# Order of the two GpSimd multiplies in each slot of a selective-scan kernel

## The reference, cut to what matters

```python
h = _L0_tok_ref(L0_tok_log_dt, L0_tok_Lambda, x, 1024)
h = jnp.concatenate([h, txt], axis=1)
# inside _L0_attn_ref, on the normalised h
dt = jax.nn.softplus(jnp.einsum('blr,dr->bld', dt_in, dt_proj_w) + dt_proj_b)
dA = jnp.exp(dt[..., None] * A)
dBx = dt[..., None] * B[:, :, None, :] * x[..., None]
h = dA_t * h + dBx_t                      # one step along the sequence
y = jnp.einsum('bdn,bn->bd', h, C_t)      # sum over the 16 states
y = jnp.moveaxis(ys, 0, 1) + D * x
```

## Time and profile before

| | us |
|---|---|
| median of 3 runs (6466.54 to 6470.77) | 6468.88 |
| the profiled execution, own time | 6470.72 |
| its span, first to last instruction | 6469.0 |
| busy in the span: PE / PEld / DVE / ACT / POOL | 5967.5 / 5445.7 / 5822.2 / 5225.1 / 5736.9 |
| mean granted TensorE clock | 0.966 |
| DMA: 478.57 MB, mean 74 GB/s | |

### The profile page before, as it was taken

How to read it: one execution, slowest core, us unless ns; L and a number is a source line. 1 busy time by engine, 2 the same in 40 slices (tenths; PEclk the granted TensorE clock), 3 DMA queues, 4 the chain that set the end, 5 groups by cost and what they waited for, 6 DMA issues and landing times. The chain is left out here.

```text
span 6469.0 us, 109402 instructions
## 1 busy us (share of the span) xinstructions
PE 5967.5 (92%) x33363; PEld 5445.7 (84%) x33363; DVE 5822.2 (90%) x4749; ACT 5225.1 (81%) x12983; POOL 5736.9 (89%) x3788
## 2 busy tenths in 40 slices
PE   4658689999999999999999999999999999999998
PEld 3433489999999999999999999999999999999997
DVE  7874599999999999999999999999999999999996
ACT  4536688888888888888888888888888888888885
POOL 2430599999999999999999999999999999999995
PEclk8769899999999999999999999999999999999999
DMA  2440121122221222221222212222212222112220
GB/s 56 97 94 0 63 76 70 68 77 85 85 74 64 79 80 84 85 72 66 74 85 85 79 61 77 79 85 84 74 64 79 79 85 84 67 66 79 85 79 32
DMA packets 96128, 478.57 MB, mean 74 GB/s; under 512 B 13089, under 2 KB 17329, under 8 KB 87410
## 3 DMA queue, kind: packets, MB, share of 16 engines
q1 hardware_dynamic: 95602, 471.63, 21.0%
HBM read 328.35 MB, written 143.24 MB: 73 GB/s over the span
## 5 line engine op out<-in xcount | busy, mean ns | idle before, releaser
L1079 POOL TENSOR_TENSOR s_ring<-s_bc,s_u_t 128x820 f32<-128x820 f32 x2048 | 3625.6, 1790 | 4.3 <-DMA s_bc<-rows_bc 4.3
L985 ACT ACTIVATE s_decay<-s_dt_t,a_neg 128x205 f32<-128x205 f32 x8192 | 3047.2, 420 | 428.9 <-DVE s_ring L1150 359.9
L882 PE MATMUL s_y_ps<-s_ring,ident 128*128 128x205 f32 x16384 | 3164.5, 343 | 142.8 <-POOL s_ring L1085 74.0
L882 PEld LDWEIGHTS s_y_ps<-s_ring,ident 128*128 128x128 f32 x16384 | 2888.4, 193 | 232.3 <-POOL s_ring L1085 139.1
L1144 DVE TENSOR_TENSOR_SCAN s_decay<-s_decay,s_ring 128x820 f32<-128x820 f32 x1216 | 2265.2, 1863 | 221.9 <-ACT s_decay L985 219.7
L1085 POOL TENSOR_TENSOR s_ring<-s_ring,s_bc 128x820 f32<-128x820 f32 x832 | 1607.3, 1932 | 55.4 <-DVE s_ring L1144 55.2
L1144 DVE TENSOR_TENSOR_SCAN s_ring<-s_decay,s_ring 128x820 f32<-128x820 f32 x832 | 1543.8, 1856 | 45.8 <-ACT s_decay L985 45.4
L915 PE MATMUL s_xch<-s_x_t,w_low 128*128 128x205 f32 x8192 | 1524.1, 338 | 0.5 <-ACT s_x_t L1025 0.2
L915 PEld LDWEIGHTS s_xch<-s_x_t,w_low 128*128 128x128 f32 x8192 | 1423.9, 190 | 32.7 <-issue 30.5
L1150 DVE TENSOR_TENSOR s_ring<-s_decay,s_bc 128x820 f32<-128x820 f32 x1216 | 1230.3, 1012 | 41.9
L307 POOL TENSOR_TENSOR t_mag<-t_mag,t_osc 128x512 f32<-128x512 f32 x128 | 167.1, 1342 | 273.0 <-ACT t_osc L293 273.0
(11 more groups left out here) (165 smaller groups left out, 4817.2 us busy)
## 6 DMA issues: line engine op xcount, KB each, us to landing
s_bc<-rows_bc SPq DMA_DIRECT2D x64, 3280.0 KB, 11.2
mixed<-t_res SPq DMA_DIRECT2D x32, 1024.0 KB, 10.0
s_x_in<-mixed SPq DMA_DIRECT2D x64, 512.0 KB
s_h<-mixed SPq DMA_DIRECT2D x64, 512.0 KB
before<-s_h SPq DMA_DIRECT2D x64, 512.0 KB
out<-s_h SPq DMA_DIRECT2D x64, 512.0 KB
s_x_in<-in_txt SPq DMA_DIRECT2D x64, 308.0 KB
s_h<-in_txt SPq DMA_DIRECT2D x64, 308.0 KB
```

Source lines behind the costliest of these rows:

```text
L882: last = nc.tensor.matmul(y_ps, ident[:, :], ring[:, c % RING, n * LEN:(n + 1) * LEN], start=False, stop=(c % 4 == 3 and n == CN - 1))
L985: last = A.activation(decay[s % 2][:, n * LEN:(n + 1) * LEN], dt_t[:, par, j, :], ACT.Exp, scale=t["a_neg"][:, j, n0 + n:n0 + n + 1])
L1079: nc.gpsimd.tensor_tensor(ring[:, s % RING, :].rearrange("p (n l) -> p n l", n=CN), bc[:, par, n0:n0 + CN, :], u_t[:, j, :].unsqueeze(1).b ...
```

## The change

Inside GpSimd's `chunk` the two parts of a slot change places: the product with C of chunk `s-3` is issued first, the inputs of chunk `s` second. The stages of `POOL_PLAN` still follow both. Nothing else is touched: the same instructions with the same operands and waits, in another order on one engine.

```diff
             def chunk(u, par, s, x, scan, after):
-                if scan:
-                    inputs(u, par, s)
                 if (s - LAG) % CHUNKS not in ON_DVE:
                     if s >= LAG and scan:
                         times_c(u, par, s - LAG)
                     if s < LAG and after:
                         times_c(u - 1, 1 - par, s - LAG + CHUNKS)
+                if scan:
+                    inputs(u, par, s)
```

## The result

The changed kernel takes **6493.74 us** (median of 14 runs, 6475.03 to 6512.86), the kernel before 6466.75 in 14 runs beside it: ratio 1.0038, 95% interval 1.0029 to 1.0048. It is 27 us slower (19 to 31 by the interval), where the prediction said 6482 (6464 to 6503), 13.6 us slower. The direction is the one forecast, and the waits that were forecast grew as they should; but as far as the traces tell, they are the smaller part of the loss. The larger part is something that the prediction did not have.

A forecast was written before the change was run, and what follows sets the result against it. Four nearly full engines, in a chain without slack through GpSimd, TensorE, ScalarE and VectorE, were taken as the bound. Late stages add 0.28 and 0.16 us, 0.44 per pair; 31 pairs give 13.6, so 6468.9 becomes 6482 (6464 to 6503).

The forecast's parts named there:

- the exits: GpSimd's product with C of chunk 18, in the even and odd entry, for which TensorE waits 0.57 and 0.19 us.
- the count of 22 steps: On GpSimd, 22 steps of inputs stand between products 28 and 18 before and after, so nothing is won there.
- `root2` 1.75 later in the even entry: GpSimd's norm stage in slot 17 gets one more step of inputs ahead of it, 1.75 us.
- ScalarE takes up 0.43: After the late shift, ScalarE's wait of 0.33 and overlap of 0.10 absorb 0.43 us, leaving 1.32 of lateness.
- Scan 3's lead: Even entry: chunk 3's inputs end 3.60 us before its scan; 3.64 new lateness may make VectorE wait 0.04 to 0.1.
- the rival of 6503: VectorE starves for late inputs at scan 3 of the even entry, up to 34 us slower; chance 0.11.
- 0.44 us a pair: Lengthening of each pair of entries from both late products of chunk 18; 13.6 us over 31 pairs.
- The 0.28 of the even entry: Lateness in us reaching GpSimd's product of chunk 18 and TensorE in the even entry.
- the 0.16 of the odd entry: Lateness in us reaching TensorE in the odd entry: 0.51, of which wait and overlap take up 0.35.
- No instruction is added or removed: Whole kernel: no DMA and no queue but GpSimd's is touched; one wait moves ahead of the inputs.
- The forecast's own band: Whole kernel's time under the main forecast, 6474 to 6492 us; chance 0.57.
- The rival "no change": GpSimd, busiest, gets no more work and ScalarE's 14% idle time takes up the lateness: 6469 us; chance 0.24.

The follow-up runs named there:

- e3: Kernel before, with the product with C issued ahead of the inputs in slots 5 to 15 alone; 6539.6 us, ratio 1.0117.
- e4: Kernel before, with the product with C issued ahead of the inputs in slots 29 to 31 and 0 to 3 only; 6532.0 us, ratio 1.0105.
- e1: Changed kernel with `root2` moved one slot earlier in GpSimd's plan, from slot 17 to 16; 6491.0 us, ratio 1.0038.
- e8: Changed kernel with TensorE's loop alone written out over 20 entries, 3 passes in place of 30; 6475.0 us, ratio 1.0014.
- e7: Kernel before with TensorE's loop alone written out over 20 entries, 3 passes in place of 30; 6459.8 us, ratio 0.9991.
- e2: Kernel before, multiplies in the old order, with `root2` moved one slot later, from slot 17 to 18; 6477.4 us, ratio 1.0017.
- e9: Kernel before, with the product with C issued ahead of the inputs in slots 4 to 28 only; 6452.9 us, ratio 0.9979.
- e12: Changed kernel with slot 31 alone put back in the old order; 6481.0 us, ratio 1.0025.
- e6: Kernel before, with the new order in slot 21 alone and `root2` moved from slot 17 to 16; 6451.4 us, ratio 0.9981.

## Why the prediction came out as it did

- **No gain at the exits, by the count of 22 steps: right.** Product 18 did not come earlier. e3 and e4 show what it costs when the count is broken (72 us where 77 were expected, 65 where the count gave 54).
- **`root2` 1.75 later in the even entry: right,** 1.76 in the rows.
- **ScalarE takes up 0.43, the block output is 1.32 later, product 18 0.26 later: right,** 1.32 and 0.25. The wait at L1034 was forecast near 80 us, 2.19 in each even entry, and is 79.6, 2.19.
- **Scan 3's lead used up to the last tenth: right.** Inputs 3 end at 3046.54 + 1.78 = 3048.32 and the scan starts at 3048.42. VectorE does not starve: the rival of 6503 has no row of waits for L1079 from 1500 to 6000 us in after.
- **0.44 us a pair, 13.6 in all: too large, by what the traces show.** After's pairs with a short turn are 0.27 us longer than before's and 0.35 longer than e1's, e8's typical pair 0.29 longer than e7's, and e2's, with only the shift late, 0.14: some 4 to 11 us. The period was to be near 177.9 and is 177.65 in pairs with a short turn. The 0.28 of the even entry is there in the rows (0.25); the 0.16 of the odd entry was not found apart. e8 against e7 gives 15.2 us in the medians, good to some 8. In e9 the wait at L1034 is 81.8 us in a kernel 13 us faster than before, so the wait alone is no price.
- **"No instruction is added or removed", and the sum that follows from it: here the working failed.** It lets nothing but waits between engines change. It has no term for TensorE's turn, though the profile of before had it in 29 places (63.3 us), 2 of them long (3.3 and 3.5). That idle time was taken as fixed by the program. It is not: the new order moved 17 of the 29 turns from 2.1 to 3.5 us. That term, some 12 us in the medians (27 - 15.2) and 28 of 36 in the profiled execution, puts the result 12 above the forecast, and from "at the edge of measurable" to clearly slower.
- **That 6493.7 lies in the range is in part luck.** The forecast's own band ended at 6492. The range went on to 6503 for a starving VectorE, which did not happen; the loss that filled it had no term.
- **The rival "no change"** had the largest share of busy time for it, GpSimd's. GpSimd's busy time hardly changed (5736.9 us before, 5740.1 after, 88% of the span), the kernel's did. The Trainium skill ("Perfetto Trace Analysis", Identifying the Most-Contended Engine) names the engine of highest occupancy as the most contended one. Here the work of that engine was unchanged and the time was not: in the steady part GpSimd is 98% busy, TensorE 97, VectorE 94, ScalarE 86, and the highest share alone did not decide.

A long turn and its extra packet have a reading in the Trainium skill ("Runtime: NRT & Kernel Launch", Instruction fetch mechanics): instructions are fetched ahead in straight order in blocks of 16 KiB, and a taken branch out of the blocks at hand must wait for a fetch. The trace agrees on two points: the stop is where the loop goes back, and q8's packets are about 16 KB each (5.55 MB / 339). That there are two kinds of turn, and one packet more in a long one, is from the runs alone. If that packet is a block beyond the loop's end, already asked for when the branch comes, it would stand ahead of the one needed; that is an argument, and no run here separates it from others.

## What to carry to other kernels

Where two streams of work share an engine's queue, count the steps between the point where the engine is let go and the point where others wait for it; a swap that left the count alone won nothing here, and whatever sits inside the loop of slots but outside the count (here a stage of a norm) is what gets later. How much that costs is not read from the wait that grows, but from the length of a period of the loop (e2, e9). Read the "issue" rows of every engine as a cost of their own, look at the longest beside the mean, and compare them before and after: a change on another engine can move them. With engines this full, turns of hardware loops were worth removing on all engines together (49 us), and on TensorE alone hardly at all; on ScalarE alone it was not tried.

## What was not expected of the hardware

- A turn of the hardware loop stops TensorE for 1.8 to 2.5 us or for 3.3 to 3.8, in the same kernel and with the same instructions around it. A kernel that adds none and removes none went from 2 long turns in 29 to 19, by the order of another engine's work.
- ScalarE stops some 2.1 us at its turn (61.4 us in 29 turns of before); VectorE and GpSimd have no such row.
- A pair of entries that begins with a long turn took 1.8 to 2.1 us more in three kernels (after, e1, e12), more than the 1.4 by which TensorE itself stands longer; in e2 it took 0.2 more.
- TensorE's stop is mostly hidden behind ScalarE's: 27 turns fewer on TensorE alone changed the time by -7 us on the kernel before and +9 on e6; 27 fewer on the other engines as well gave 49 us.
- 27 turns fewer on TensorE also took 46 instruction packets off q8 (322 to 276).
